# GRU and expert layer on one core: input product and b_hn written into PSUM by ScalarE and VectorE instead of being added by TensorE

## The chip, the cores and the metric

One core of a Trainium2 chip runs the whole kernel. The time is the device time of one execution in microseconds (us), median of several runs. TensorE (PE in the profile) multiplies into PSUM, VectorE (DVE), ScalarE (ACT) and GpSimd (POOL) work element by element, SyncE (SP) issues most DMAs. The engines run side by side, each through its own list of instructions in order, and wait for each other through semaphores.

## The reference

A GRU runs over x (4 sequences of 512 steps, width D = 512), its states pass through a layer of 4 experts, and x is added:

```python
def cell(h, x):
    gi = x @ W_ih + b_ih
    gh = h @ W_hh + b_hh
    i_r, i_z, i_n = jnp.split(gi, 3, axis=-1)
    h_r, h_z, h_n = jnp.split(gh, 3, axis=-1)
    r = jax.nn.sigmoid(i_r + h_r)
    z = jax.nn.sigmoid(i_z + h_z)
    n = jnp.tanh(i_n + r * h_n)
    h_new = (1.0 - z) * n + z * h
    return (h_new, h_new)
...
# each token: softmax over the 2 best of 4 experts; each expert takes its 512
# best-scored tokens: y = gelu(tok @ W1[e]) @ W2[e] * p, scattered back by addition
x = x + _L0_ffn_ref(_L0_cond_ref(cond, x, W_ih, W_hh, b_ih, b_hh), Wg, bg, W1, W2)
```

h_n holds its own bias b_hn, the last third of b_hh, which is inside the product with r.

## The kernel before

**Recurrence.** Each of the 4 sequences is cut into 16 segments of 32 steps, and all 64 segments run side by side as 64 columns (COLS). 8 steps of approach (BURN), then 32 steps, then 32 again whose states count: 72 steps, i = 0 to 71. A step needs gates = W_hh x state: 512 inputs are KD = 4 blocks k of 128 partitions, the outputs are 4 blocks j times 3 gates g (r, z, n). Block j of the gates has a PSUM bank of its own, `gate_ps[:, j, g, :]`, 192 of its 512 columns.

Numbers are split into a high and a low f16 part. In **rough** steps (i < ROUGH = 20) only high x high is multiplied: 48 products of 64 columns. In **exact** steps the list ORDER gives (HIGH, j, k), six products (high and low weights times the state's high part), and (LOW, j, k), three (high weights times its low part): 144 products in an order written by hand. TensorE's `unit` issues them, waiting for `high_ready` and `low_ready`/`last_low_ready` of block k. Its last product of block j raises `gates_mm`.

**Input product.** x W_ih is made in four chunks of 8 steps, 12 tiles of 128x512 each (m = 0 to 3 for r, 4 to 7 for z, 8 to 11 for n). The first chunk comes from f32 products before step 0. The rest is made by 432 f16 **fills** of 512 columns, spread over the steps up to 22 (`fill`, 18 a step; in rough steps 13, 2, 2 and 1 ahead of each k). ScalarE takes each tile out of PSUM (`keep_tile`). The n gates go into `gi` as f32. The r and z gates go to the ring `gi_full`, and VectorE splits them into two f16 parts, `gi_rz`, with `rz_high` (L1128) and `rz_low` (L1135).

**Adding it.** In each step TensorE's `inject` (L469, L472) opens each bank: the diagonal matrix `diag` (the scale) times gi_rz's high part of r and z (128 columns), in exact steps also times its low part, and `bhn_parts` times `bhn_unit` (64 columns) for b_hn. `inject(j)` waits for the reset of block j of the step before (`rn_done`), which is the last reader of the bank. In rough steps b_hn is added by VectorE's reset (L1248, three operands); in exact ones reset is L1245.

**The state.** ScalarE: sigmoid of r and z of block j (L779), tanh (L784), in the order sig 0, 1, 2, tanh 0, 1, sig 3, tanh 2, 3. VectorE, in an order written by hand (`exact`, `rough`): `reset` (r times h_n), `candidate_in` (L1253), `one_less_z` (L1257), `blend` (L1264, the new state's high part), in exact steps `keep_state` (L1269, the f32 state) and the low part of blocks 2 and 3 (`low_part`, L1288). GpSimd: `carry` (L952, z times old state) and the low part of blocks 0 and 1 (L960). `other_work` puts further VectorE work behind a step's list: x_low (L1146), whh_low (L1211, at the steps of WHH_AT), the splits of the input product, and the router's weights in step 10. ScalarE takes the tiles out behind its step, and in steps 29 to 40 and 45 to 48 squares a piece of W1 for its peak (L799).

**After the recurrence** come the router, a search for each expert's best tokens, and the experts; the change touches there only which PSUM banks two small results use.

Lines the prediction names besides: L434 and L424 are the first tiles' f32 products, L451 the fills, L459 the gate products, L479 the router's logits, L740 and L745 `keep_tile`, L753 `first_tile_high`, L1179 the diagonal.

Of the kernel before, what the change touches and what calls it, by code (L numbers as in the profile page):

```python
# [23 lines left out]
P = 128  # L24
# [12 lines left out]
def gru_moe(nc, x, x_t, cond_t, w_ih, w_hh, b_ih, b_hh, b_hn, wg, bg, w1, w2, hs_rows, out):  # L37
# [18 lines left out]
    with ExitStack() as ctx:  # L56
# [3 lines left out]
        def sem(name):  # L60
# [12 lines left out]
        gi_rz = big[:, :].bitcast(F16).rearrange("p (n j q) -> p n j q", n=NC_, j=KD)[:, :, :, 0:4 * GCOLS].rearrange(  # L73
            "p n j (i g c) -> p n j i g c", i=2, g=2)
# [58 lines left out]
        diag = sb("diag", [P, P], BF16)  # L133
# [38 lines left out]
        def of_first(q):  # L172
# [61 lines left out]
        lg_sum = ps[:, 4, L * 2 * E:2 * L * 2 * E].rearrange("p (l e) -> p l e", l=L)  # L234
        lg_again = ps[:, 5, 0:NT * E].rearrange("p (n e) -> p n e", n=NT)
        gate_ps = ps[:, 0:4, 0:3 * COLS].rearrange("p j (g c) -> p j g c", g=3)

        names = """small_loaded out_init consts_pool consts_dve bias_ready
             gi_mm gi_high gi_low gi_kept diag_ready sig_done gates_known gi_known x_known wih_high wih_split whh_high x_high x_split peak_ready peak_known chain whh_ready zh_done warmed high_ready state_done low_ready last_low_ready gates_mm rn_done
            candin_ready tanh_done ocand_done start_saved check_a worst_ready worst_mm flag_ready  # L240
            gru_over turned bhn_clear bhn_loaded bhn_split wg_split lg_mm lg_kept sq_done probs_in probs_stored group_made rows_copied rows_stored steps_made exp_in exp_done
# [1531 lines left out]
```

## Time and profile before

| | us |
|---|---|
| time, median of 3 runs | 836.3 (836.11 to 837.08) |
| the profiled execution | 836.27 |
| its span, first to last instruction | 834.5 |
| TensorE busy, matmuls | 803.0 (96%) |
| VectorE busy | 619.8 (74%) |
| ScalarE busy | 421.1 (50%) |
| GpSimd busy | 179.9 (22%) |
| mean granted TensorE clock | 0.987 |

The recurrence ends at about 442 us, the experts fill the rest. "Busy" of TensorE counts each matmul from its start to a modelled end, so matmuls overlap. In a timeline a row merges neighbouring instructions of a kind: start, time from the first's start to the last's end, and their number. [brackets] at the end of a row give the engine's idle time before it and who ended it.

### The profile page before, as it was taken

What the parts mean: (1) busy time and instruction counts of PE and PEld (TensorE: products, weight loads), DVE (VectorE), ACT (ScalarE), POOL (GpSimd) and SP (SyncE); (2) the same over time, 40 slices, a digit from 0 to 9 for tenths busy, and PEclk for the clock granted to TensorE, in tenths of its full rate; (3) what the DMA queues carried; (4) which work ended last, traced back from release to release, by engine and by line L of the source; (5) the groups of instructions that cost most, each with busy time, mean ns of one, the idle gap of its engine ahead of it and who ended that gap; (6) DMA issues with size and microseconds to landing.
All of it is one profiled execution on the core that took longest, in us unless ns stands there. A gap on an engine that the chain in (4) does not pass through costs nothing.

```text
span 834.5 us, 28320 instructions
## 1 busy us (share of the span) xinstructions
PE 803.0 (96%) x11781; PEld 528.0 (63%) x11782; DVE 619.8 (74%) x2113; ACT 421.1 (50%) x885; POOL 179.9 (22%) x459
## 2 busy tenths in 40 slices
PE   7999999999999999999995799999999999999996
PEld 3446556679999999999994444454445444444442
DVE  6979899878888888888888879767666676755300
ACT  0677666645566556554455448252835184417400
POOL 1002222123433334333330010121012101210011
PEclk9999999999999999999997899999999999999998
DMA  9810000000111010000001943471347224630022
GB/s 336 323 48 2 2 2 3 2 3 4 54 60 50 17 42 5 4 4 5 5 4 33 269 156 119 135 226 27 113 139 194 57 101 151 171 81 1 1 26 26
DMA packets 24286, 62.64 MB, mean 75 GB/s; under 512 B 4386, under 2 KB 4386, under 8 KB 22308
## 3 DMA queue, kind: packets, MB, share of 16 engines
q1 hardware_dynamic: 19312, 51.42, 18.1%
q0 software_dynamic: 3584, 8.42, 5.5%
q8 instruction: 87, 1.43, 0.7%
q10 hardware_dynamic: 1268, 1.08, 0.4%
q14 instruction: 35, 0.29, 0.1%
HBM read 52.50 MB, written 12.62 MB: 78 GB/s over the span
## 4 chain that ended last, share of the span: by engine, by line
PE 92%; DVE 5%; issue 1%; DMA 1%; ACT 0%; POOLq 0%; DVEq 0%
PE ps L459 29%; PE ps L666 20%; PE ps L680 20%; PE ps L451 10%; PE ps L469 3%; PE ps L434 3%; PE ps L424 2%; PE ps L600 1%; PE ps L653 1%; DVE big L1541 1%; PE ps L472 1%; DMA wa<-in_x_t 1%; DVE halves L1264 1%; DVE wa L1253 1%; PE ps L644 0%
## 5 line engine op out<-in xcount | busy, mean ns | idle before, releaser
L459 PE MATMUL ps<-halves,wa 128*128 128x64 f16 x8448 | 289.1, 193 | 1.4 <-DVE halves L1264 1.2
L459 PEld LDWEIGHTS ps<-halves,wa 128*128 128x128 f16 x8448 | 271.2, 98 | 20.2 <-DVE halves L1264 4.2
L680 PE MATMUL ps<-big 128*128 128x512 f16 x768 | 166.9, 379 | 0.0
L666 PE MATMUL ps<-hx,big 128*128 128x512 f16 x768 | 166.9, 379 | 0.0
L779 ACT ACTIVATE wa<-ps,un_gates 128x128 f32<-128x128 f32 x288 | 100.1, 365 | 111.0 <-PE ps L459 100.6
L680 PEld LDWEIGHTS ps<-big 128*128 128x128 f16 x768 | 75.1, 98 | 89.9
L666 PEld LDWEIGHTS ps<-hx,big 128*128 128x128 f16 x768 | 74.8, 98 | 90.0 <-issue 0.2
L784 ACT ACTIVATE wa<-wa,un_gates 128x64 f32<-128x64 f32 x288 | 97.4, 344 | 53.0 <-DVE wa L1253 48.9
L451 PE MATMUL ps<-hx,wb 128*128 128x512 f16 x432 | 106.9, 379 | 1.2 <-issue 1.1
L861 ACT ACTIVATE hx<-ps,un_hid_in 128x512 f32<-128x512 f32 x64 | 43.6, 682 | 109.2 <-PE ps L666 106.9
L1264 DVE SCALAR_TENSOR_TENSOR halves<-ocand,neg_scale,wa 128x64 f16<-128x64 f32 (+1 forms) x288 | 80.6, 280 | 4.4 <-issue 0.5
L1495 DVE SCALAR_TENSOR_TENSOR big<-wa,scale,big 128x2048 f16<-128x2048 f32 x28 | 65.3, 2350 | 21.1 <-ACT big L847 21.1
L1245 DVE TENSOR_TENSOR wa<-ps,wa 128x64 f32<-128x64 f32 x208 | 45.9, 221 | 43.4 <-ACT wa L779 43.4
L1253 DVE TENSOR_TENSOR wa<-wa,big 128x64 f32<-128x64 f32 x288 | 71.6, 249 | 5.1
L1629 DVE SCALAR_TENSOR_TENSOR big<-hx,hid_scale,big 128x512 f16<-128x512 f32 x64 | 47.8, 750 | 35.2 <-ACT big L864 29.0
L847 ACT ACTIVATE big<-wa,scale 128x2048 f16<-128x2048 f32 x28 | 54.8, 1988 | 34.1 <-DVEq L1483 34.1
L1441 DVE TENSOR_REDUCE chunk_peak<-wa 128x1 f32<-128x2048 f32 x28 | 62.3, 2279 | 4.5 <-DMA wa<-in_w 4.5
L469 PE MATMUL ps<-big,diag 128*128 128x128 f16 x496 | 63.5, 219 | 0.8 <-DVE wa L1245 0.4
L1257 DVE SCALAR_TENSOR_TENSOR ocand<-wa 128x64 f32<-128x64 f32 x288 | 63.5, 220 | 0.0
L451 PEld LDWEIGHTS ps<-hx,wb 128*128 128x128 f16 x432 | 37.9, 98 | 35.8 <-issue 1.9
L1018 POOL DMA_INDIRECT out<-hx,idx_out x16 | 29.0, 1815 | 136.1 <-DVE hx L1635 136.1
L952 POOL TENSOR_TENSOR wa<-wa,hx 128x64 f32<-128x64 f32 x128 | 40.9, 320 | 79.9 <-ACT wa L779 75.2
(221 smaller groups left out, 791.4 us busy)
## 6 DMA issues: line engine op xcount, KB each, us to landing
wa<-in_w SPq DMA_DIRECT2D x28, 1024.0 KB, 5.2
hs_rows<-big SPq DMA_DIRECT2D x8, 512.0 KB, 6.3
big<-in_w_hh SPq DMA_DIRECT2D x4, 768.0 KB, 19.6
wb<-in_w SPq DMA_DIRECT2D x12, 256.0 KB, 2.6
big<-in_w_ih SPq DMA_DIRECT2D x2, 1024.0 KB, 12.5
hx<-in_x_t SPq DMA_DIRECT2D x2, 1024.0 KB, 16.5
big<-in_w_ih ACTq DMA_DIRECT2D x2, 512.0 KB, 6.6
wa<-in_x_t SPq DMA_DIRECT2D x2, 512.0 KB, 6.2
```

The source lines that it names most:

```text
L451: mm = pe.matmul(ps[:, gi_bank(tile), :], wih_parts[:, w, k, m * P:(m + 1) * P], x_parts[:, q, t, k, :], start=(left == 0), stop=(left == ...
L459: mm = pe.matmul(gate_ps[:, j, g, :], whh_parts[:, k, w, (4 * g + j) * P:(4 * g + j + 1) * P], halves[:, src, k, h, :], start=False, stop= ...
L469: pe.matmul(gate_ps[:, j, 0:2, :], diag[:, :], gi_rz[:, c, j, part, :, cols], start=(part == HIGH), stop=False, skip_group_check=True)
L666: mm = pe.matmul(ps[:, m % 2, :], w1p[:, w, k, m * P:(m + 1) * P], tokT[:, t, k, :], start=(k == 0 and n == 0), stop=(k == KD - 1 and n == 2))
L680: mm = pe.matmul(ps[:, 2 + g % 2, :], hid[:, h, k, g * P:(g + 1) * P], w2p[:, w, k, :], start=(k == 0 and n == 0), stop=(k == KH - 1 and n ...
L779: act.activation(rz[:, j, :, :], gate_ps[:, j, 0:2, :], ACT.Sigmoid, scale=un_gates[:, 0:1]).then_inc(S["sig_done"], 1)
L784: act.activation(cand[:, j, :], cand_in[:, j, :], ACT.Tanh, scale=un_gates[:, 0:1]).then_inc(S["tanh_done"], 1)
L1253: dve.tensor_tensor(cand_in[:, j, :], rn[:, j, :], gi_n(j), ALU.add).then_inc(S["candin_ready"], 1)
L1257: dve.scalar_tensor_tensor(ocand[:, j, :], rz[:, j, 1, :], -1.0, cand[:, j, :], ALU.add, ALU.mult).then_inc(S["ocand_done"], 1)
L1264: dve.scalar_tensor_tensor(high_of(j), old(ocand_, j), neg_scale[:, 0:1], old(zh_, j), ALU.mult, ALU.add).then_inc(S["high_ready"], 1)
L1441: dve.tensor_reduce(chunk_peak[:, c:c + 1], stage[:, c * CHUNK:(c + 1) * CHUNK], AX.X, ALU.max, apply_absolute_value=True).then_inc(S["chu ...
L1495: dve.scalar_tensor_tensor(w_parts[which][:, LOW, cols], stage[:, cols], scale[:, which:which + 1], w_parts[which][:, HIGH, cols], ALU.mul ...
```

## The change

TensorE no longer opens the banks. The r and z input product stays f32 in `gi_rz`, written by `keep_tile` directly, two gates of a step side by side, so `gi_full`'s ring, `rz_high` and `rz_low` go, and with them `inject`, `diag` and the split of b_hn. What `inject` added is now written into the gate banks before the products, which accumulate onto it: a **seed**, two instructions, `gi_rz` times the column `seed_s` (128 columns of a block) and b_hn (64 columns).

Steps 0 to 23: VectorE writes the seeds of step i + 1 block by block at the end of its list of step i (`seed_next`, eight instructions), ahead of `other_work` in the rough steps. TensorE does all 18 fills of a rough step first, then the products block by block, j outside and k inside, each block behind `seeded_early`.

Steps 24 to 71: ScalarE writes them. Blocks 0 to 2 have two sets of banks (0 to 2 and 5 to 7) used in turn, and after its last tanh of step i ScalarE seeds blocks 0 to 2 of step i + 2 (`seed_most`, 384 and 192 elements) and block 3 of step i + 1 (`seed_last`, 128 and 64). In step 23 it seeds all that steps 24 and 25 need. The squares come behind the seeds.

```diff
-        gate_ps = ps[:, 0:4, 0:3 * COLS].rearrange("p j (g c) -> p j g c", g=3)
+        GATES = 3 * COLS
+        gate_banks = (ps[:, 0:KD - 1, 0:GATES], ps[:, 5:5 + KD - 1, 0:GATES])
+        last_gates = ps[:, KD - 1, 0:GATES]
...
-        INJECT = 2
-        ORDER = ((INJECT, 0, 0), (INJECT, 1, 0), (HIGH, 1, 0), (INJECT, 2, 0), (HIGH, 0, 0), (HIGH, 2, 0),
-                 (INJECT, 3, 0), (HIGH, 0, 1), (HIGH, 1, 1), (LOW, 1, 0), (HIGH, 2, 1), (LOW, 2, 0),
...
+        ORDER = ((HIGH, 1, 0), (HIGH, 0, 0), (HIGH, 2, 0), (HIGH, 0, 1), (HIGH, 1, 1), (LOW, 1, 0),
...
-        FILLS = (13, 2, 2, 1)
-        FILL_STEP = sum(FILLS)
+        FILL_STEP = 18
...
             def gates_rough(src, i):
-                n = filled(i)
-                for k in range(KD):
-                    fill(n + sum(FILLS[:k]), n + sum(FILLS[:k + 1]))
-                    if k == 0 and i % STEPS_C == 0:
-                        pe.wait_ge(S["gi_high"], 8 * (i // STEPS_C) + 8)
-                    pe.wait_ge(S["high_ready"], made(i) + k + 1)
-                    for j in range(KD):
-                        if k == 0:
-                            inject(j, *place(i), (HIGH,), KD * i)
-                        unit(HIGH, j, k, src, (HIGH,), k == KD - 1)
+
+                fill(filled(i), filled(i + 1))
+                for j in range(KD):
+                    pe.wait_ge(S["seeded_early"], 2 * (KD * i + j + 1))
+                    for k in range(KD):
+                        pe.wait_ge(S["high_ready"], made(i) + k + 1)
+                        unit(0, HIGH, j, k, src, (HIGH,), k == KD - 1)
...
+                    if j not in begun:
+                        begun.add(j)
+                        if early:
+                            pe.wait_ge(S["seeded_early"], 2 * (2 * half_steps + j + 1))
+                        elif j == KD - 1:
+                            pe.wait_ge(S["last_seeded"], half_steps + (2 - 2 * FILLED))
+                        elif j == ORDER[0][1]:
+                            pe.wait_ge(S["seeded"], half_steps + (2 - 2 * FILLED))
...
+            def seed_most(bank, rows_of, before):
+
+                act.wait_ge(S["rn_done"], before)
+                act.activation(gate_banks[bank][:, :, 0:2 * COLS], rows_of(slice(0, KD - 1)), ACT.Copy,
+                               scale=seed_s[:, 0:1]).then_inc(S["seeded"], 1)
+                act.activation(gate_banks[bank][:, :, 2 * COLS:GATES],
+                               bhn_s[:, 0:KD - 1].unsqueeze(2).to_broadcast([P, KD - 1, COLS]), ACT.Copy
+                               ).then_inc(S["seeded"], 1)
...
+            def seed_ahead(i):
+
+                if i + 2 < FIRST + L:
+                    seed_most(bank_of(i + 2), rows_at(i + 2), KD * (i + 2))
+                if i + 1 < FIRST + L:
+                    seed_last(rows_at(i + 1), KD * (i + 2))
...
             for i in range(FIRST + L):
-                step(KD * i)
+                step(KD * i, bank_of(i))
+                if i >= FILLED:
+                    seed_ahead(i)
...
+                if i + 1 == FILLED:
+                    act.wait_ge(S["gi_kept"], 12 * NC_)
+                    act.wait_ge(S["seeds_known"], 1)
+                    seed_most(bank_of(FILLED), rows_at(FILLED), KD * FILLED)
+                    seed_ahead(i)
...
+            def seed(i, j):
+
+                c = (i // STEPS_C + CHUNK_ORDER[0]) % NC_
+                dve.tensor_scalar(gates_of(0, j)[:, 0:2 * COLS], gi_rz[:, c, j, i % STEPS_C, :], seed_s[:, 0:1], None,
+                                  ALU.mult).then_inc(S["seeded_early"], 1)
+                dve.tensor_copy(gates_of(0, j)[:, 2 * COLS:GATES], bhn_s[:, j:j + 1].to_broadcast([P, COLS])
+                                ).then_inc(S["seeded_early"], 1)
...
-                         (low_part, 3))
+                         (low_part, 3), *((seed_next, j) for j in range(KD)))
...
-                         (one_less_z, 2), (blend, 2), (one_less_z, 3), (blend, 3), (other_work, 0))
-                for f, n in ahead:
-                    f(n)
+                         (one_less_z, 2), (blend, 2), (one_less_z, 3), (blend, 3),
+                         *((seed_next, j) for j in range(KD)), (other_work, 0))
```

## Rows read from the trace of the kernel before

**Rows 1.** The page, the chain that ended last: share of the span by engine.

```profile
PE 92%; DVE 5%; issue 1%; DMA 1%; ACT 0%; POOLq 0%; DVEq 0%
```

**Rows 2.** Busy us of each engine by stretch, granted TensorE clock, DMA.

```profile
60.00:170.00 110.00, 109.56 (x1374) 66.45 (x1371) 98.95 (x386) 72.05 (x195) 24.15 (x81) 1.00 0.01 2
170.00:202.00 32.00, 31.01 (x782) 26.36 (x780) 23.58 (x109) 14.92 (x41) 8.95 (x26) 1.00 0.02 4
202.00:260.00 58.00, 57.85 (x1814) 56.11 (x1811) 48.86 (x260) 34.48 (x108) 23.09 (x72) 1.00 0.16 50
```

**Rows 3.** Timeline of TensorE, rough steps: start us, us, engine, line, tiles, count.

```profile
61.25 2.97 PE L451 MATMUL ps<-hx,wb 128*128 128x512 f16 x13
...
66.76 2.97 PE L451 MATMUL ps<-hx,wb 128*128 128x512 f16 x13
```

**Rows 4.** Timeline of TensorE, exact steps 20 and 24.

```profile
172.03 3.84 PE L459 MATMUL ps<-halves,wa 128*128 128x64 f16 x126
...
203.00 0.28 PE L469 MATMUL ps<-big,diag 128*128 128x128 f16 x2
...
203.46 0.35 PE L459 MATMUL ps<-halves,wa 128*128 128x64 f16 x6
...
204.28 3.88 PE L459 MATMUL ps<-halves,wa 128*128 128x64 f16 x126
```

**Rows 5.** Timeline of VectorE, a rough step whose list starts late.

```profile
72.69 0.28 DVE L1248 SCALAR_TENSOR_TENSOR wa<-ps,bhn_s,wa 128x64 f32<-128x64 f32 x1
...
76.18 0.42 DVE L1128 CAST big<-gi_full 128x512 f16<-128x512 f32 x1
76.63 0.69 DVE L1135 TENSOR_TENSOR big<-gi_full,big 128x512 f16<-128x512 f32 x1
```

**Rows 6.** Timeline of VectorE, exact steps 24 and 25.

```profile
203.84 0.29 DVE L1264 SCALAR_TENSOR_TENSOR halves<-ocand,neg_scale,wa 128x64 f16<-128x64 f32 x1
...
206.76 0.22 DVE L1245 TENSOR_TENSOR wa<-ps,wa 128x64 f32<-128x64 f32 x1 [0.76 <-ACT wa L779]
...
210.59 0.41 DVE L1288 TENSOR_TENSOR halves<-carried,halves 128x64 f16<-128x64 f32 x2
211.75 0.23 DVE L1245 TENSOR_TENSOR wa<-ps,wa 128x64 f32<-128x64 f32 x1 [0.76 <-ACT wa L779]
```

**Rows 7.** Timeline of ScalarE, an exact step with a square.

```profile
229.36 0.35 ACT L784 ACTIVATE wa<-wa,un_gates 128x64 f32<-128x64 f32 x1 [0.60 <-DVE wa L1253]
229.62 0.61 ACT L799 ACTIVATE wa<-wb 128x512 f32<-128x512 f32 x1
230.14 0.19 ACT L799 ACTIVATION_READ_ACCUMULATOR wa<-wb 128x1 f32 x1
231.32 1.16 ACT L779 ACTIVATE wa<-ps,un_gates 128x128 f32<-128x128 f32 x3 [0.99 <-PE ps L459]
```

**Rows 8.** The page, costliest groups: busy us, mean ns, idle before.

```profile
L847 ACT ACTIVATE big<-wa,scale 128x2048 f16<-128x2048 f32 x28 | 54.8, 1988 | 34.1 <-DVEq L1483 34.1
```

**Rows 9.** Timeline of TensorE, where the fills begin.

```profile
50.57 8.15 PE L451 MATMUL ps<-hx,wb 128*128 128x512 f16 x37 [1.14 <-issue]
```

**Rows 10.** VectorE's groups by line and shape, rough steps: busy us, mean ns.

```profile
L1248 DVE SCALAR_TENSOR_TENSOR wa<-ps,bhn_s,wa 128x64 f32<-128x64 f32 x76 | 21.1, 278 | 6.6 <-ACT wa L779 6.5
...
L1211 DVE SCALAR_TENSOR_TENSOR wa<-big,scale,wa 128x512 f16<-128x512 f32 x12 | 9.0, 750 | 0.0
```

**Rows 11.** Timeline of VectorE, the diagonal before step 0.

```profile
50.38 0.29 DVE L1179 TENSOR_SCALAR diag<-ident,un_gi 128x128 bf16<-128x128 f32 x1
```

**Rows 12.** Timeline of TensorE, first products of steps 20 and 23.

```profile
167.05 4.06 PE L451 MATMUL ps<-hx,wb 128*128 128x512 f16 x18
...
191.71 0.28 PE L469 MATMUL ps<-big,diag 128*128 128x128 f16 x2
```

**Rows 13.** Timeline of TensorE, behind the router's search.

```profile
474.07 2.53 PE L644 MATMUL ps<-tok_group,gi_full 128*128 128x4 f16 x16 [2.50 <-DVE gi_full L1599]
```

**Rows 14.** TensorE's busy us and granted clock behind that.

```profile
475.00:480.00 5.00, 5.00 (x19) 0.50 0.94 333
```

More of the change, by code:

```diff
@@ L463, in unit @@
                     mm.then_inc(S["gates_mm"], 1)
-            def inject(j, c, cols, parts, steps):
-                pe.wait_ge(S["rn_done"], steps + j + 1)
-                for part in parts:
-                    pe.matmul(gate_ps[:, j, 0:2, :], diag[:, :], gi_rz[:, c, j, part, :, cols],
-                              start=(part == HIGH), stop=False, skip_group_check=True)
-                if LOW in parts:
-                    pe.matmul(gate_ps[:, j, 2, :], bhn_parts[:, j * P:(j + 1) * P], bhn_unit[:, :], start=False,
-                              stop=False, skip_group_check=True)
             def logits(i):
@@ L542, in _, with run @@
             logits(FIRST + L).then_inc(S["lg_mm"], 1)
-            def run(base, low_base, steps):
+            def run(base, low_base, half_steps):
                 for c in range(NC_):
@@ L806, in _, with run @@
                     x_high(i // STEPS_C + 1, i % STEPS_C)
-            def run(steps, n):
-                with act.Fori(0, n // 2) as i:
-                    for u in range(2):
-                        step(steps + 8 * i + 4 * u)
+                if i + 1 == FILLED:
[3 more added lines that the diff above has]
+                    seed_ahead(i)
+            def run(steps):
+                for c in range(NC_):
+                    with act.Fori(0, STEPS_C // 2) as i:
+                        for u in range(2):
+                            base = steps + KD * STEPS_C * c + 8 * i + 4 * u
+                            rows_of = lambda j: gi_rz[:, c, j, bass.ds(2 * i + u, 1), :].rearrange(
+                                "p j o q -> p (j o) q" if isinstance(j, slice) else "p o q -> p (o q)")
+                            seed_most(1 - u, rows_of, base + KD)
+                            seed_last(rows_of, base + KD)
+                            step(base, 1 - u)
             def exponents(count):
@@ L1206, in whh_low @@
+            for j in range(KD):
+                seed(0, j)
             def whh_low(n):
@@ L1228, in w1_peak, with step @@
                 dve.tensor_reduce(peak[:, W1:W1 + 1], sq[:, :], AX.X, ALU.max).then_inc(S["w_peak"], 1)
-            def step(gi_n, after, src, base, low, moved=False, ahead=(), between=(), bias_added=True):
+            def step(gi_n, after, src, base, low, bank, moved=False, between=(), following=None):
                 dst = 1 - src
@@ L1337, in _ @@
                     after = lambda j, i=i: hs[:, j, i - FIRST + 1, :]
-                ahead, between = [], []
-                if i < FILLED:
-                    for t in range(split_by(i - 1), split_by(i)):
-                        if TILES[t][1] < 8:
-                            (ahead if s == STEPS_C - 1 else between).append((rz_high, t))
-                            (ahead if i == FILLED - 1 else between).append((rz_low, t))
+                between = []
                 if 1 <= s <= KD and q < 2:
@@ L1351, in _ @@
                     between.append((w1_peak, 0))
-                step(lambda j, c=c, cols=cols: gi[:, c, j, 2, cols], after, i % 2, KD * i, i >= ROUGH - 1, moved, ahead, between,
-                     i >= ROUGH)
+                step(lambda j, c=c, cols=cols: gi[:, c, j, 2, cols], after, i % 2, KD * i, i >= ROUGH - 1, bank_of(i), moved,
+                     between, i + 1 if i + 1 < FILLED else None)
             def run(steps):
```

174 lines of the change are left out of this document (62 added, 112 removed).

## The prediction

> **Names.** Step i is step i of the recurrence, i = 0 to 71; steps 0 to 19 are rough, 20 to 71 exact. E(i) is the start of the last gate product of step i on TensorE. A "slot" is the time from one instruction's start to the next one's on the same engine when nothing is waited for.
>
> **What bounds the kernel now.** I read the chain that ended last first, then the busy shares by stretch, then the timelines of TensorE, VectorE and ScalarE over single steps. The chain is 92% TensorE [rows 1], which invites the sum "every product removed is time gained". The stretches [rows 2] say the same: TensorE is busy for 109.6 of 110 us in the rough steps and for 57.9 of 58 in exact ones. The busy figure of a matmul is a pipelined 0.19 us while products start 0.03 us apart, so it hides gaps of 0.1 us. One has to look inside a step.
>
> Rough step [rows 3]: 13 fills in 2.97 us, the last of them 0.38, are 0.216 us each from start to start. 126 products of 64 columns in 3.84 us [rows 4], the last 0.19, are 0.0292 each. The period is 66.76 - 61.25 = 5.51 us. 18 fills are 3.89, 48 products 1.40, so the four input products take the rest, 0.22. There is no gap: TensorE bounds these steps. VectorE is close behind. Its 16 instructions for the state run from 72.69 to 76.18 when it starts late, 3.49 us, then come rz_high and rz_low, 0.42 and 0.69 busy [rows 5], and a piece of other splitting.
>
> Exact step [rows 4]: here a gap shows. Step 20's last 126 products, for which VectorE is nowhere late, take 3.84 us. Step 24's and all later ones take 3.88. So 0.04 us is waited for in every steady step, in the middle of the products, and 0.2 us more between the input products and the first unit (203.00 plus two groups at 0.14, then 203.46). What TensorE waits for in the middle is the low half of the state's last quarter. VectorE starts a step's list with reset 0 at 206.76 and issues the last pair of low parts at 210.59 for 0.41 us [rows 6]; in between it is never idle. The circle is: VectorE's list, 4.24 us to the end of low part 3 at 211.00; then 0.75, of which 0.03 until TensorE starts the unit (LOW, 0, 3), 0.06 until that completes gate 0, and the rest for sigmoid 0 and its two hand-overs; then reset 0 again at 211.75. 4.99 us, the step. VectorE's list therefore sets the exact steps together with TensorE, and the input products lie in TensorE's wait for the state.
>
> **The change, part by part.**
>
> *Exact steps 25 to 71 (47).* 12 products go (8 of 128 columns, 4 of 64). A group of three starts 0.14 behind the one before (two of 128 columns at twice 0.0292, one of 64), the four are 0.56 us. Without them TensorE waits for high part 0 just the same, then for high part 1 (blend 1, 203.84 to 204.13 [rows 6], used from 204.28 now [rows 4]), then for low parts 2 and 3. The unit (LOW, 0, 3) begins when low part 3 is there, at the same place of the circle. All 0.56 us turns into waits: **0**. If the low parts were not what is waited for, high part 1 would still hold the step to 0.12 below the present one, 4.88.
>
> *ScalarE's seeds.* Each of these steps gets four ACTIVATEs of 384, 192, 128 and 64 elements. A tanh of 64 elements with its scale from memory is 0.35 us and the next instruction starts after 0.26; a square of 512 with an immediate scale is 0.61 [rows 7]. 2048 elements with a scale from memory are 1.988 [rows 8], so an element is (1.988 - 0.35) / 1984 = 0.00083 us, and the fixed part is 0.29 with the scale from memory and 0.19 without. The four are 0.61, 0.35, 0.40 and 0.24; with 0.09 of overlap each, slots of 0.52, 0.26, 0.31 and 0.15: 1.24 us. Writing PSUM from ScalarE is in no row; I bound the four by 1.05 (0.05 cheaper each) and 1.6 (0.09 dearer each). From the last tanh to the next sigmoid 0 there are 231.32 - 229.36 = 1.96 us. From tanh 3 a plain step needs 0.26 + 1.24 = 1.50 and keeps 0.46. In 16 steps (29 to 40, 45 to 48) a square with its accumulator read lies there too, 0.52 + 0.19 = 0.71 [rows 7]: 2.21 us, 0.25 too many. Sigmoid 0 is on the circle without slack, so each costs 0.25: **+4.0** (bounds +1.0 and +9.8). Queued behind the square are the three sigmoids, and VectorE's whole list waits for them.
>
> The rows hold no ACTIVATE into PSUM. The Trainium skill ("ScalarE: Activation LUTs", "Step-by-step: what each stage is for") says an ACTIVATE into PSUM is faster than one into SBUF. No row of before shows it; by it the term would lie at the lower bound, +1.0.
>
> *The start.* rz_low 0 to 3 leave VectorE's list and three rz_high leave ScalarE's; TensorE's idle of 1.14 us before the fills [rows 9] was for the last x_low, which now ends some 1.8 us earlier, so the fills begin at 49.43. 42 of them and 48 products put E(0) at 49.43 + 9.07 + 1.40 = 59.9, against 61.25 [rows 3].
>
> *Rough steps.* TensorE alone would need 3.89 + 1.40 = 5.29. VectorE gives up rz_high and rz_low but takes eight seeds, behind the blends and ahead of its other work. Its state list gets shorter since reset becomes a two-operand instruction, 0.22 [rows 6] for 0.278 [rows 10]; with the hand-overs 3.49 becomes 3.30. A seed of 128 elements is a multiply by a column into PSUM. The nearest rows are the diagonal, 128 elements in 0.29 [rows 11], and three-operand instructions: 0.278 for 64 elements, 0.750 for 512 [rows 10], so 0.00105 us an element and 0.345 for 128. Slots are 0.08 under the busy time: 0.21 or 0.27. The copy of 64 has a slot of 0.14 (0.22 busy, as a reset). A pair is 0.35 to 0.41, and 0.49 if writing PSUM costs the overlap of the first. I take 0.41, the element rate that most rows have; four pairs are 1.63 (bounds 1.3 and 2.0). Other work, whh_low or x_low at 0.75 busy [rows 10], is a slot of about 0.70 in 18 steps, double in step 1, and 1.54 more in step 10: 15.5 in all. So VectorE needs 3.30 + 1.63 + 0.70 = 5.63 in a usual step, more than TensorE's 5.29 and more than 5.51. It becomes the bound, and its other work now stands between the seeds and the next reset.
>
> The row of the diagonal alone would allow two elements a cycle. The Trainium skill ("VectorE: DVE Perf Modes", "Why PSUM operands drop a tier") says that an fp32 instruction with a PSUM operand runs at one. By the row four pairs are 1.40, by the page 1.63.
>
> Sum: the gates of a rough step are now completed one after the other over the last 1.05 us before E, so VectorE's list of 3.30 begins some 0.3 us before E(0) and, with waits for the later gates, ends near 3.1 behind it, at 63.0. Eighteen more steps at 3.30 + 1.63 are 88.7, their other work 14.7, the shifted step 7 0.4: 166.8. Seeds (1.63), hand-over (0.08) and the last unit's 12 products (0.35) put E(19) 2.06 later, 168.9. The fills of step 20 follow it; before they began at 167.05 [rows 12]. **+1.9**, start included (bounds -6.5, TensorE-bound, and +9).
>
> *Steps 20 to 24.* The exact list on VectorE is free again at 210.59 + 0.33 [rows 6], 2.95 us behind E(25) = 203.00 + 4.99 - 0.03, and the seeds of the next step come only behind it. TensorE's first units need pairs 1 and 0, 0.82 more and 0.05 for the hand-over: 3.80 behind E. 18 fills (3.89) cover that, 12 fills (2.59) before step 22 don't, and nothing covers it before step 23. A step's 144 products are 4.2. Step 20: its list starts 0.29 behind E(19), so 0.29 + 4.16 + 0.87 + 4.25 = 9.6. Step 21: 3.89 + 4.2 = 8.1. Step 22: 3.80 + 4.25 = 8.05. The three are 25.75 against 191.71 - 167.05 = 24.7 [rows 12]. Step 23: 8.05. Step 24 is seeded by ScalarE, behind tanh 3 of step 23 (its slot ends 1.7 behind E), two slots and the hand-over: its products start 2.6 behind E and it takes 6.8. The two are 14.85 against 203.00 - 191.71 = 11.3, in which the splits rz_high and rz_low made TensorE wait. Together **+4.6** (bounds +3.5 and +6).
>
> *The clock.* TensorE stands idle for about 3.7 us before step 23. In this trace an idle of 2.50 us [rows 13] was followed by a granted clock of 0.50, the 1.2 GHz level, for over 4 us of work [rows 14]. Half of 4.2 us is **+2.1** (bounds 0 and +5, were it to happen before step 24 too).
>
> The router and the experts are unchanged. Total: 1.9 + 4.6 + 2.1 + 4.0 = +12.6. The profiled execution took 836.27 us (span 834.5 and 1.8 around it), the median of the three runs is 836.3, so one baseline serves: **848.9 us**.
>
> **Rivals.**
>
> *A. TensorE does bound the exact steps.* Then 47 x 0.56 = 26 us go, less what ScalarE allows: at 4.45 a step the room of 1.96 is 1.41 and its 1.50 sets 4.53, so 22 us: 827. For it: the chain [rows 1]. Against: the 0.04 us wait in each steady step [rows 4]. It decides from 12.6 / 47 = 0.27 us a step. Chance 0.08.
>
> *B. The seeds on VectorE are cheap.* At 1.3 us for four pairs VectorE needs 5.3 and TensorE bounds the rough steps: E(19) = 59.9 + 19 x 5.29 = 160.4, 8.5 us below my sum, and the total is 840, 838 with the clock kept up, 835 with ScalarE at its lower bound as well. Chance 0.12.
>
> *C. Seeds are dear on both engines.* 2.0 us on VectorE adds 7.4, 1.5 on ScalarE adds 4.2: 860. Chance 0.12.
>
> *D. Only the high parts hold the exact steps*, at 4.88: 47 x 0.12 = 5.6 less, 843. Chance 0.06.
>
> *E. The clock falls in the exact steps.* TensorE would idle 0.7 us of 5. At the lower level 144 products take 8.4 and a step over 8.4, +3.4 us in each of 47: 1009. Against it: the stretch from 170 to 202 us, in which TensorE idles for 0.99 us, has a clock of 1.00 [rows 2]. The Trainium skill ("TensorE: Matmul & The Clock Gate", "HAM oscillation — how this bites in real kernels") describes a clock that falls again and again where bursts of matmuls are parted by waits; the trace so far sides against it for waits this short. Chance 0.02.
>
> **How the numbers follow.** The forecast has 0.60, by itself 841 to 857. Below 837 lie A and a part of B (0.11), above 860 E and half of C (0.08): range 837 to 860. 0.2% (1.7 us) is about what a measurement can tell. Faster by more: A and 0.02 of B, 0.10. Within: 0.05 from B's lower end. Slower: 0.85.
>
> **What would show it.** Exact plain steps still 5.0 us apart with TensorE waiting at two or three places; square steps 0.2 to 0.3 longer; rough steps near 5.6 with VectorE never idle; a hole of some 3.7 us before step 23 and 2.6 before step 24; a clock of 0.50 behind the hole. Wrong if exact steps fall clearly under 5.0, or rough steps come every 5.3 us.

## The result and the profile after

The changed kernel took 843.48 us (842.39 to 845.57), the kernel before beside it 836.48: a ratio of 1.0086 (95% interval 1.0063 to 1.0109). It is slower by 7.0 us; the forecast was 12.6 slower. The profiled execution took 842.39 us with a span of 840.6, 6.1 more than the profiled one of before. Its parts, read at the same places of both traces:

| | forecast | measured |
|---|---|---|
| start and rough steps, to the fills of step 20 | +1.9 | +0.1 |
| steps 20 to 24, clock left out | +4.6 | +4.4 |
| low clock in step 23 | +2.1 | +1.55 |
| exact steps 25 to 71, products and squares | +4.0 | -0.4 |
| router and experts | 0 | +0.5 |

The page's chain that ended last, which had 92% on TensorE [rows 1] (the exact steps take 4.99 us in both kernels, so these shares alone say little of what bounds them):

```profile
PE 61%; DVE 28%; ACT 6%; issue 3%; DMA 1%; POOLq 0%; DVEq 0%
```

TensorE's timeline, steps 20 to 24 (start, us, engine, line, tiles, count, idle before it and who ended it); the last row is step 26:

```profile
167.17 4.06 PE L446 MATMUL ps<-hx,wb 128*128 128x512 f16 x18
172.18 4.36 PE L454 MATMUL ps<-halves,wa 128*128 128x64 f16 x144 [0.96 <-DVE ps L1177]
...
188.40 4.36 PE L454 MATMUL ps<-halves,wa 128*128 128x64 f16 x144 [1.16 <-DVE ps L1177]
196.51 5.91 PE L454 MATMUL ps<-halves,wa 128*128 128x64 f16 x144 [3.74 <-DVE ps L1177]
204.86 4.36 PE L454 MATMUL ps<-halves,wa 128*128 128x64 f16 x144 [2.45 <-DVE halves L1246]
...
214.50 4.69 PE L454 MATMUL ps<-halves,wa 128*128 128x64 f16 x144 [0.29 <-DVE halves L1246]
```

The fills of step 20 begin at 167.17 where they began at 167.05 [rows 12]. Then four waits stand there, of 0.96, 1.16, 3.74 and 2.45 us; the first three end with a seed of VectorE (L1177 is its copy of b_hn into PSUM). Beside the fourth the profile names a blend of step 23, which ends at 204.71; but step 24's first products need the first block only, whose blend was done at 202.64, and ScalarE's seed for blocks 0 to 2, the row below, ends at 204.72. So ScalarE's seed ends that wait, as forecast; e1's trace names it. Step 23's 144 products take 5.91 us and not 4.36. The steady step's take 4.69: 0.33 us of waiting inside, and 0.29 before it. The next row of that kind is 4.99 us on (219.49), as before.

```profile
204.41 0.31 ACT L747 ACTIVATE ps<-bhn_s 128x192 f32<-128x192 f32 x1
```

TensorE's granted clock there (stretch, length, busy us and counts by engine, clock, DMA):

```profile
196.50:199.00 2.50, 2.49 (x60) 2.50 (x61) 0.62 (x4) 0.00 (x0) 0.00 (x0) 0.66 0.02 7
199.00:202.00 3.00, 3.00 (x81) 3.00 (x79) 0.97 (x5) 1.32 (x5) 0.80 (x3) 0.72 0.00 0
...
209.00:440.00 231.00, 217.49 (x6752) 205.04 (x6748) 191.32 (x1017) 181.28 (x586) 90.12 (x276) 1.00 0.08 23
```

Behind the wait of 3.74 us a part of the work runs at the lower level, 1.2 GHz. Behind the wait of 2.45 it doesn't, and the exact steps keep 1.00 although TensorE waits 0.6 us in each.

VectorE's timeline, a rough step:

```profile
76.32 0.22 DVE L1222 TENSOR_TENSOR wa<-ps,wa 128x64 f32<-128x64 f32 x1
...
79.70 0.35 DVE L1175 TENSOR_SCALAR ps<-big,seed_s 128x128 f32<-128x128 f32 x1
79.96 0.22 DVE L1177 COPY ps<-bhn_s 128x64 f32<-128x64 f32 x1
80.08 0.34 DVE L1175 TENSOR_SCALAR ps<-big,seed_s 128x128 f32<-128x128 f32 x1
...
81.22 0.74 DVE L1139 SCALAR_TENSOR_TENSOR hx<-hx,scale 128x512 f16<-128x512 f32 x1
81.88 0.22 DVE L1222 TENSOR_TENSOR wa<-ps,wa 128x64 f32<-128x64 f32 x1
```

The list for the state is 3.38 us (3.30 foreseen), the four pairs 81.22 - 79.70 = 1.52 (1.63 foreseen; a pair has slots of 0.26 and 0.12), other work 0.66 (0.70): 5.56, with no gap on VectorE longer than 0.11 us.

ScalarE's timeline, the first exact step with a square, which answers to [rows 7]:

```profile
235.49 0.35 ACT L779 ACTIVATE wa<-wa,un_gates 128x64 f32<-128x64 f32 x1 [0.60 <-DVE wa L1235]
235.74 0.57 ACT L745 ACTIVATE ps<-big,seed_s 128x384 f32<-128x384 f32 x1
236.25 0.31 ACT L747 ACTIVATE ps<-bhn_s 128x192 f32<-128x192 f32 x1
236.50 0.35 ACT L754 ACTIVATE ps<-big,seed_s 128x128 f32<-128x128 f32 x1
236.79 0.20 ACT L756 ACTIVATE ps<-bhn_s 128x64 f32<-128x64 f32 x1
236.94 0.61 ACT L796 ACTIVATE wa<-wb 128x512 f32<-128x512 f32 x1
237.46 0.19 ACT L796 ACTIVATION_READ_ACCUMULATOR wa<-wb 128x1 f32 x1
237.55 1.05 ACT L774 ACTIVATE wa<-ps,un_gates 128x128 f32<-128x128 f32 x3
...
240.48 0.35 ACT L779 ACTIVATE wa<-wa,un_gates 128x64 f32<-128x64 f32 x1 [0.60 <-DVE wa L1235]
```

From tanh 3 to sigmoid 0 it is 2.06 us where a plain step has 1.96: sigmoid 0 comes 0.10 late. Yet tanh 3 to tanh 3 is 240.48 - 235.49 = 4.99.

VectorE's timeline, reset 0 and the first one_less_z of the plain step ahead of it and of this one:

```profile
232.85 0.22 DVE L1222 TENSOR_TENSOR wa<-ps,wa 128x64 f32<-128x64 f32 x1 [0.76 <-ACT wa L774]
...
233.87 0.23 DVE L1239 SCALAR_TENSOR_TENSOR ocand<-wa 128x64 f32<-128x64 f32 x1
...
237.93 0.22 DVE L1222 TENSOR_TENSOR wa<-ps,wa 128x64 f32<-128x64 f32 x1 [0.84 <-ACT wa L774]
...
238.86 0.23 DVE L1239 SCALAR_TENSOR_TENSOR ocand<-wa 128x64 f32<-128x64 f32 x1
```

Reset 0 is 5.08 behind the one before, but one_less_z 0 is 4.99 behind its own: the five instructions between them take 0.93 us instead of 1.02, because small waits among them close up.

### The profile page after: what moved, and what is told of

The parts are those of the page before. It is cut to its first block, busy times and chain, and to the rows that moved or that the text cites. A ratio compares the mean times of both kernels' runs of the same rounds, so it can differ in the third digit from the quotient of the medians.

```text
span 840.6 us, 27308 instructions
## 1 busy us (share of the span) xinstructions
PE 788.2 (94%) x11077; PEld 501.6 (60%) x11078; DVE 617.1 (73%) x2237; ACT 476.7 (57%) x1072; POOL 190.5 (23%) x459
## 4 chain that ended last, share of the span: by engine, by line
PE 61%; DVE 28%; ACT 6%; issue 3%; DMA 1%; POOLq 0%; DVEq 0%
PE ps L643 20%; PE ps L657 20%; PE ps L454 12%; DVE wa L1235 6%; DVE halves L1246 5%; DVE wa L1222 4%; PE ps L429 3%; DVE ocand L1239 3%; DVE ps L1175 3%; ACT wa L774 2%; PE ps L419 2%; PE ps L446 2%; ACT wa L796 1%; DVE ps L1177 1%; DVE wa L1189 1%
## 5 line engine op out<-in xcount | busy, mean ns | idle before, releaser
L454 PE MATMUL ps<-halves,wa 128*128 128x64 f16 x8448 | 275.8, 194 | 24.6 <-DVE halves L1246 15.0
L454 PEld LDWEIGHTS ps<-halves,wa 128*128 128x128 f16 x8448 | 259.8, 98 | 47.7 <-DVE halves L1246 20.3
L774 ACT ACTIVATE wa<-ps,un_gates 128x128 f32<-128x128 f32 x288 | 103.8, 365 | 56.3 <-PE ps L454 47.3
L1222 DVE TENSOR_TENSOR wa<-ps,wa 128x64 f32<-128x64 f32 x288 | 63.0, 219 | 57.1 <-ACT wa L774 57.1
L446 PE MATMUL ps<-hx,wb 128*128 128x512 f16 x432 | 97.0, 379 | 0.1
L446 PEld LDWEIGHTS ps<-hx,wb 128*128 128x128 f16 x432 | 40.7, 98 | 46.4 <-issue 0.6
L960 POOL TENSOR_TENSOR wa<-wa,halves 128x64 f32<-128x64 f32 x80 | 34.9, 455 | 84.5 <-ACT wa L774 84.4
```

The lines of the kernel that those rows point to most:

```text
L446: mm = pe.matmul(ps[:, gi_bank(tile), :], wih_parts[:, w, k, m * P:(m + 1) * P], x_parts[:, q, t, k, :], start=(left == 0), stop=(left == ...
L454: mm = pe.matmul(gates_of(bank, j)[:, g * COLS:(g + 1) * COLS], whh_parts[:, k, w, (4 * g + j) * P:(4 * g + j + 1) * P], halves[:, src, k, ...
L774: act.activation(rz[:, j, :, :], gates_of(bank, j)[:, 0:2 * COLS].rearrange("p (g c) -> p g c", g=2), ACT.Sigmoid, scale=un_gates[:, 0:1]) ...
L960: pool.tensor_tensor(zh[:, j, :], rz[:, j, 1, :], before(j), ALU.mult).then_inc(S["zh_done"], 1)
L1222: dve.tensor_tensor(rn[:, j, :], gates_of(bank, j)[:, 2 * COLS:GATES], rz[:, j, 0, :], ALU.mult).then_inc(S["rn_done"], 1)
```

## The experiments

The theory after the result: (1) in the exact steps VectorE's list to the end of low part 3 sets the period; (2) in the rough steps it is VectorE's whole list with the seeds; (3) steps 20 to 24 pay for seeds that stand behind everything else, and once more by the clock. Rivals: TensorE still bounds the exact steps and another thing took the 26 us back; ScalarE does; the clock is an affair of the whole stretch. A difference in us below is between medians; "changed" stands for 843.5.

**e1, the holes filled.** Dummy products of 512 columns ahead of steps 22, 23 and 24:

```
+ KEPT_WARM = {22: 5, 23: 16, 24: 10}
+ if i in KEPT_WARM:
+     pe.wait_ge(S["gi_kept"], 45)
+     for _ in range(KEPT_WARM[i]):
+         pe.matmul(ps[:, 4, :]..., onesb, onesb..., start=True, stop=True)
```

> The changed kernel, with products nobody reads (512 columns, another bank) in TensorE's waits: 5 ahead of step 22, 16 ahead of step 23, 10 ahead of step 24. Clock theory: the granted clock stays at 1.00 over steps 22 to 24, step 23's 144 products take 4.36 us instead of 5.91, the holes keep their length, and the time falls by 1.5 us to some 841. The changed kernel's spread from run to run (842.4 to 845.6) should shrink too, if it is the clock's. Rival, that the long step 23 has another cause (its waits for high and low parts): it stays at 5.9 and the time at 843.

841.57 us, ratio 1.0057 (1.0040 to 1.0074). TensorE's timeline, steps 23 and 24:

```profile
192.82 3.62 PE L515 MATMUL ps<-onesb 128*128 128x512 bf16 x16
196.73 4.36 PE L455 MATMUL ps<-halves,wa 128*128 128x64 f16 x144 [0.29 <-DVE ps L1183]
...
203.55 4.36 PE L455 MATMUL ps<-halves,wa 128*128 128x64 f16 x144 [0.30 <-ACT ps L753]
```

The products of step 23 begin where they did (196.73 for 196.51), so the hole is not TensorE's doing, and take 4.36 for 5.91. What the idle time had cost was the clock: 1.55 us, 1.9 by the medians. The four times of e1 lie within 0.7 us, those of the changed kernel within 3.2; that fits a loss by the clock that differs from one execution to the next (e8 has a trace with a larger one).

**e2 and e3, low part 2 by GpSimd**, in the changed kernel and in the one before. VectorE's list loses one of two low parts, the circle of theory (1):

```
- LOW_BY = "PPDD"
+ LOW_BY = "PPPD"
-  (one_less_z, 3), (keep_state, 2), (blend, 3), (keep_state, 3), (low_part, 2),
+  (one_less_z, 3), (keep_state, 2), (blend, 3), (keep_state, 3),
```

> The changed kernel, with the low part of block 2 made by GpSimd instead of VectorE in all exact steps. Theory (VectorE's list up to low part 3 sets the exact steps, TensorE has 0.5 us of waits in each): low part 3 comes 0.13 earlier, the next limit is high part 1, so steps of 4.88 instead of 4.99 and 47 x 0.11 = 5 us less: 838. Rival 1, TensorE bounds the exact steps: no change, 843. Rival 2, GpSimd's extra work slows VectorE's own instructions on the way they share: 843 to 848.

> The kernel before, with the same move of low part 2 to GpSimd. Theory: TensorE waits there in the middle of a step for 0.04 us only, so at most 47 x 0.04 = 1.9 us can come off: 834.5 to 836. If it gained as much as the changed kernel does by the same move (5 us), TensorE's input products would be free in both, and what the change saves on TensorE would be worth nothing even with a shorter VectorE list.

Both slower: 847.16 (ratio 1.0131, 1.0114 to 1.0148) and 841.28 (1.0057, 1.0040 to 1.0073), 3.7 us over the changed kernel and 4.4 over the one before. VectorE's timeline of e2:

```profile
350.98 0.23 DVE L1222 TENSOR_TENSOR wa<-ps,wa 128x64 f32<-128x64 f32 x1 [0.76 <-ACT wa L774]
...
354.03 0.35 DVE L1239 SCALAR_TENSOR_TENSOR ocand<-wa 128x64 f32<-128x64 f32 x1
...
354.70 0.27 DVE L1251 SCALAR_TENSOR_TENSOR hx<-ocand,neg_scale,wa 128x64 f32<-128x64 f32 x1
355.07 0.23 DVE L1270 TENSOR_TENSOR halves<-hx,halves 128x64 f16<-128x64 f32 x1
356.05 0.22 DVE L1222 TENSOR_TENSOR wa<-ps,wa 128x64 f32<-128x64 f32 x1 [0.76 <-ACT wa L774]
```

Two costs stand against the gain. Low part 3 waits for keep_state 3 to finish (355.07, 0.10 after its end), which low part 2 had covered. And one_less_z 3 takes 0.35 us where it takes 0.21, beside GpSimd's extra work. The list was meant to get shorter and got longer: from reset 0 to the end of low part 3 it is 355.30 - 350.98 = 4.32 us, where the changed kernel has 4.23 (e8 shows its rows), and the period is 5.07 for 4.99. The period follows that end, as theory (1) says, but the move did not test its gain. That both kernels react alike, one with the input products and one without, speaks for one bound in both.

**e4 and e10, more work on ScalarE.** One or two further copies, into a spare SBUF tile, ahead of the seeds (e4: 192 and 64 elements, slots 0.25 and 0.15; e10: the one of 64):

```
  def seed_ahead(i):
+     act.wait_ge(S["spared"], spares[0])
+     act.activation(spare[:, 0:KD - 1, :], bhn_s..., ACT.Copy).then_inc(S["spared"], 1)   # e4 alone
+     act.activation(spare[:, KD - 1, :], bhn_s..., ACT.Copy).then_inc(S["spared"], 1)
```

> The changed kernel, with two more ScalarE copies of b_hn (192 and 64 elements, into SBUF) ahead of the seeds in steps 23 to 71, 0.41 us of ScalarE a step. Theory (from tanh 3 to sigmoid 0 there are 1.96 us and 0.10 of slack behind them; tanh, seeds and square take 0.26 + 1.20 + 0.61 = 2.06): plain steps 0.26 + 1.20 + 0.41 = 1.87, no change, 4.99; the 16 square steps 2.47, 5.40 each, so 6.6 us more in all: 850. Without any slack, as the prediction had it, square steps would take 5.50. Rival, that ScalarE is not near the limit even with squares: no change.

> The changed kernel with one more copy of 64 elements (0.24 us, a slot of 0.15) on ScalarE ahead of the seeds. With two copies (0.40) the 16 steps that have a square took 5.54 us, the others 4.99; without any all take 4.99 and the first square step 5.08. Theory (in square steps ScalarE's own loop, from tanh 3 over seeds and square to sigmoid 0 and back to tanh 3, is as long as VectorE's, so every added nanosecond shows): 5.54 - 0.25 = 5.29 in square steps, 16 x 0.30 = 4.8 us, 848.3. Rival (there is about 0.1 us of slack left that the square didn't use, and the two copies also changed the order of arrivals): 5.04 to 5.14, 844.5 to 846. Rival (no slack at all but no jump either, the loop is 4.99 + 0.15): 5.14, 845.9.

e4 took 852.3 us (ratio 1.0184, 1.0165 to 1.0202), e10 847.36 (1.0140, 1.0121 to 1.0160). ScalarE's timeline of e10, a square step:

```profile
240.63 0.35 ACT L786 ACTIVATE wa<-wa,un_gates 128x64 f32<-128x64 f32 x1 [0.80 <-DVE wa L1242]
...
245.93 0.35 ACT L786 ACTIVATE wa<-wa,un_gates 128x64 f32<-128x64 f32 x1 [0.80 <-DVE wa L1242]
```

Plain steps stay at 4.99 in both: there ScalarE has room for 0.40 us. Square steps become 5.54 and 5.28 to 5.30: 16 x 0.55 = 8.8 and 16 x 0.30 = 4.8, the medians say 8.8 and 3.9. (One of the 16 takes 5.65 in the changed kernel, 5.90 in e4 and still 5.65 in e10, so the steps themselves give 8.5 and 4.5.) The step follows the dose one to one (0.25 for 0.25), but the line through both points meets 5.14 at no dose, where 4.99 is measured. So the square steps stand at an edge: up to the seeds and the square as they are nothing shows, and 0.15 us more costs 0.30. The extra 0.15 goes with an order of arrivals (candidate_in 1 takes 0.37 us for 0.22 and tanh 1 waits 0.19 for it, in both). The traces show GpSimd beside it: its third multiply begins 0.02 to 0.04 us ahead of candidate_in 1 in e10 and e4 (some 238.56 for 238.59 in e10), in the changed kernel 0.09 behind it (238.67 for 238.58), and 0.37 - 0.22 is the 0.15. It fits what GpSimd did to one_less_z 3 in e2, but it was not tried.

**e5, ScalarE seeds steps 20 to 23**, behind tanh 3 of the step before; VectorE keeps steps 0 to 19:

```
- between, i + 1 if i + 1 < FILLED else None)
+ between, i + 1 if i + 1 < ROUGH else None)
+ if ROUGH <= i + 1 < FILLED:
+     seed_early(i + 1)
```

> The changed kernel, but the banks of steps 20 to 23 are written by ScalarE (four copies, 1.20 us, behind tanh 3 of the step before) and VectorE writes those of steps 0 to 19 only. Theory (the holes before steps 22 and 23 are VectorE's list plus two seed pairs, and the low clock in step 23 follows from the hole of 3.74 us): the first two copies end 0.25 + 0.50 + 0.25 us behind the start of tanh 3, so the hole before step 23 becomes about 2.45 us as it is before step 24, step 23's products take 4.36 us and not 5.91, and step 20's and 22's fill waits go: 5.0 to 5.6 us less than the changed kernel, about 837. Rival (the low clock comes from the light load of the whole stretch and not from the long hole): step 23 stays at 5.9 us, about 839. Rival (the place of the seeds doesn't matter since the products of these steps wait for the state): no change, 842.4.

839.29 us, ratio 1.0030 (1.0018 to 1.0042), 4.2 less than changed. TensorE's timeline, steps 22 to 24:

```profile
183.42 2.75 PE L446 MATMUL ps<-hx,wb 128*128 128x512 f16 x12
186.04 4.36 PE L454 MATMUL ps<-halves,wa 128*128 128x64 f16 x144
192.85 5.91 PE L454 MATMUL ps<-halves,wa 128*128 128x64 f16 x144 [2.45 <-ACT ps L768]
201.21 5.73 PE L454 MATMUL ps<-halves,wa 128*128 128x64 f16 x144 [2.45 <-DVE halves L1265]
```

The waits before steps 20 and 22 are gone and the one before 23 is 2.45, as the theory said. But both steps behind a wait of 2.45 us now run partly at the low clock, which my expectation excluded. Step 23 does so behind a single wait: TensorE's timeline marks none from 167.24 to 190.40, and the granted clock was 1.00 up to 194 us and 0.50 behind that. In the changed kernel the same wait before step 24, behind a step that had itself run partly at the low level, left the clock alone. So the length of the wait does not decide, and no run here shows what does. The first rival of the expectation met both of its numbers, 5.9 us and 839. Its reason, the light load of the whole stretch in place of one long hole, stays open: e1 and e9 fill the holes and with them the stretch, so they show that TensorE's idle time there costs the clock, and not which part of it.

The two slow steps cost 1.55 + 1.37 = 2.9 us in this execution, where the changed kernel lost 1.55, so by the traces the new place of the seeds is worth some 1.4 us more than the 4.2. The profiled execution is one of the slower ones of e5, 1.3 us above its median.

**e6, VectorE's seeds merged**: four instructions where there were eight (384 and 192 elements, then 128 and 64).

```
+ dve.tensor_scalar(gate_banks[0][:, :, 0:2 * COLS], gi_rz[:, c, 0:KD - 1, i % STEPS_C, :], seed_s[:, 0:1], None, ALU.mult)
+ dve.tensor_copy(gate_banks[0][:, :, 2 * COLS:GATES], bhn_s[:, 0:KD - 1]...)
  (and the same two for last_gates)
```

> The changed kernel, but VectorE writes the banks of steps 0 to 23 with four instructions (three units' 384 and 192 elements, then the last unit's 128 and 64) where it had eight. From the slots of 0.255 for 128 and 0.13 for 64 elements and 0.00105 us an element for a multiply by a column, the four are about 1.17 us and the eight 1.53. Theory (from the fifth rough step on VectorE's list of 3.38 + 1.53 + other work sets the period of 5.56 us): it needs 5.2 now, TensorE's fills and products set 5.29, and 14 steps give back 0.27 each and the hole of step 10 a part: 4 to 5 us less than the changed kernel, about 838.5. Rival (the period is set by TensorE and the hand-over at the step's start, since the first gate's bank now comes later than before): 842.4 or up to 2 more.

839.26 us, ratio 1.0032 (1.0019 to 1.0045), 4.2 less. VectorE's timeline:

```profile
79.96 0.61 DVE L1176 TENSOR_SCALAR ps<-big,seed_s 128x384 f32<-128x384 f32 x1
80.48 0.35 DVE L1178 COPY ps<-bhn_s 128x192 f32<-128x192 f32 x1
80.75 0.34 DVE L1182 TENSOR_SCALAR ps<-big,seed_s 128x128 f32<-128x128 f32 x1
81.00 0.22 DVE L1184 COPY ps<-bhn_s 128x64 f32<-128x64 f32 x1
81.12 0.74 DVE L1139 SCALAR_TENSOR_TENSOR hx<-hx,scale 128x512 f16<-128x512 f32 x1
```

The seeds take 81.12 - 79.96 = 1.16 us for 1.52, and the rough step falls to TensorE's 5.29. Step 20's fills begin at 162.93 instead of 167.17. Theory (2) holds: in the rough steps VectorE was the bound. On TensorE the products of two steps start 86.27 - 80.98 = 5.29 us apart.

**e7, the products put back.** Twelve idle products per step of about the removed sizes, at their old places in TensorE's list:

```
+ for n, (h, j, k) in enumerate(ORDER):
+     if not early:
+         for _ in range((2, 1, 0, 1)[n] if n < 4 else 0):
+             for cols in (127, 127, COLS):
+                 pe.matmul(ps[:, 4, 384:384 + cols], onesb[:, :], onesb[:, 0:cols], start=True, stop=True)
```

> The changed kernel, with products of the removed ones' number and about their size put back in steps 24 to 71, at their old places in TensorE's list (two groups of three ahead of the first unit, one behind the first unit, one behind the third; 127, 127 and 64 columns; they read a constant and write to columns that nothing uses). 12 of them were 0.56 us a step in the kernel before. Theory (the removed products lay in TensorE's waits for the high and low parts, VectorE's list sets the step): the step stays 4.99, in all 842.4 and at most 1 us more. Rival A of the forecast (TensorE bounds the step): up to 0.56 us in each of 48 steps, 869. Half-way rival (a part of the 0.56 us, the group ahead of the second high part, no longer fits since the seeds changed the arrival of the gates): 0.1 to 0.2 a step, 847 to 852.

843.39 us, ratio 1.0081 (1.0068 to 1.0095), 0.1 beside the changed kernel's 843.48. TensorE's timeline:

```profile
301.66 3.88 PE L454 MATMUL ps<-halves,wa 128*128 128x64 f16 x126
...
306.65 3.88 PE L454 MATMUL ps<-halves,wa 128*128 128x64 f16 x126
```

The pattern of [rows 4] is back, 3.88 us for 126 products included, and the step is still 4.99 (306.65 - 301.66). 576 products cost nothing. Rival A is out: TensorE does not bound these steps, however full its list looks.

**e8, one more copy on VectorE**, of 64 elements, between keep_state 3 and low part 2 of steps 24 to 71:

```
+ def spare_copy(_):
+     dve.wait_ge(S["spared"], base // KD - FILLED)
+     dve.tensor_copy(spare[:, :], bhn_s[:, 0:1].to_broadcast([P, COLS])).then_inc(S["spared"], 1)
- (blend, 3), (keep_state, 3), (low_part, 2),
+ (blend, 3), (keep_state, 3), (spare_copy, 0), (low_part, 2),
```

> The changed kernel with one more copy of 64 elements into a spare tile on VectorE, between keep_state 3 and low_part 2 of steps 24 to 71 (a slot of 0.13 us). Theory (the circle of the exact step is VectorE's list to the end of low part 3, then the unit that uses it, sigmoid 0 and reset 0): 0.13 us a step in 47 steps, 6 us more than the changed kernel, 848.5 and a period of 5.12. Rival D of the forecast (the high parts hold the step, at 4.88, and the low parts come 0.1 us early): at most 0.02 to 0.03 a step, 843.5. Rival (tanh 0 behind sigmoid 2 on ScalarE closes the circle): no change, 842.4.

845.25 us, ratio 1.0110 (1.0092 to 1.0128), 1.8 over changed: neither of my numbers. VectorE's timeline of the changed kernel, then that of e8:

```profile
212.81 0.23 DVE L1222 TENSOR_TENSOR wa<-ps,wa 128x64 f32<-128x64 f32 x1 [0.76 <-ACT wa L774]
...
216.63 0.41 DVE L1270 TENSOR_TENSOR halves<-carried,halves 128x64 f16<-128x64 f32 x2
217.80 0.22 DVE L1222 TENSOR_TENSOR wa<-ps,wa 128x64 f32<-128x64 f32 x1 [0.76 <-ACT wa L774]
```

```profile
218.23 0.18 DVE L1272 COPY spare<-bhn_s 128x64 f32<-128x64 f32 x1
218.34 0.35 DVE L1277 TENSOR_TENSOR halves<-carried,halves 128x64 f16<-128x64 f32 x2
219.44 0.23 DVE L1223 TENSOR_TENSOR wa<-ps,wa 128x64 f32<-128x64 f32 x1 [0.76 <-ACT wa L775]
```

The copy has a slot of 0.11 us, but the pair of low parts behind it shrinks from 0.41 to 0.35: low part 3 had been waiting for keep_state 3, and the copy fills that wait. The pair ends 0.04 to 0.05 later in the step and the period is 5.03, 0.04 more; 47 x 0.04 = 1.9, the 1.8 of the medians. The profiled execution took 847.01, 1.8 above the median: there step 23's products, behind a wait of 3.75 us (3.74 in the changed kernel), took 6.62 us and not 5.91. The period follows the end of low part 3, as theory (1) says, and from there to the next reset 0 it is 0.76 (217.80 - 217.04) and 0.75 us (219.44 - 218.69). I had priced the copy, not what it does to that end.

**e9, the three together**: e5, e6 and ten idle products ahead of steps 23 and 24.

> The changed kernel with three edits together: ScalarE writes the banks of steps 20 to 23 (alone 4.2 us less than the changed kernel), VectorE's seeds of steps 0 to 19 are four instructions in place of eight (alone 4.2 us less), and 10 idle products of 512 columns stand ahead of steps 23 and 24. With the seeds moved alone both holes of 2.45 us were there and steps 23 and 24 took 5.91 and 5.73 us. Theory (the three costs are separate, and the clock falls for the idle of the two holes together): steps 23 and 24 take 4.36 us, 2.9 us less, and the sum is 843.5 - 4.2 - 4.2 - 2.9 = 832.2, faster than the kernel before (836.9) by 0.5%. Rival (the gains overlap, as the rough steps end earlier but the state of step 20 then waits for something else): 835 to 837. Rival (the clock falls elsewhere instead): 834.5 to 835.5.

832.67 us (831.86 to 833.29), ratio 0.9952 (0.9938 to 0.9965): faster than the kernel before by 4.2 us and than the changed one by 10.8. TensorE's timeline, steps 23 and 24:

```profile
187.16 4.36 PE L455 MATMUL ps<-halves,wa 128*128 128x64 f16 x144 [0.30 <-DVE halves L1278]
191.36 2.32 PE L515 MATMUL ps<-onesb 128*128 128x512 bf16 x10
193.97 4.36 PE L455 MATMUL ps<-halves,wa 128*128 128x64 f16 x144 [0.29 <-DVE halves L1278]
```

Steps 23 and 24 take 4.36 again, and the sum of the single gains, 832.2, was met within 0.5. So the loss of the change lay in the rough steps' list and in steps 20 to 24, and the time can be had back in both; e9's two holes are still there, filled with products that nobody reads.

## Why the prediction was right, and where its sizes were off

**Exact steps, the products: right.** Their removal was put at 0, and e7 shows it from the other side. (The unit of [rows 4] at 203.46, called step 24's there, is step 25's; no term changes by it.) The measured time lies on rival D's 843, by chance: D wants exact steps of 4.88, and they take 4.99. Low part 3 is on the circle: e8 moved the period by just what it moved its end, and from there to reset 0 it is 0.75 to 0.76 us in both kernels. Only the last piece was drawn too simply, as the squares showed.

**The squares: the step that failed, +4.0 for 0.** It is most of the error: without this term the forecast is 844.9. Two things were wrong in "0.52 + 0.19" and "sigmoid 0 is on the circle without slack". The accumulator read is 0.19 busy but its slot is 0.09 (237.46 to 237.55): I had taken the busy time for the slot, which I had not done with any other instruction. That leaves 0.10 to 0.15. And sigmoid 0 has that much room: reset 0 came 0.09 late and one_less_z 0 on time. One_less_z 0 waits for tanh 0, which stands behind sigmoid 2 on ScalarE, and tanh 0 was on time too (238.50, 0.95 behind sigmoid 0 where a plain step has 1.05). Sigmoid 2 waits for gate 2, complete 27 products after gate 0, so the circle closes through gate 2 and tanh 0, and reset 0 lies 0.09 us beside it. The lateness did not add up: the first square step is 5.08 from reset 0 to reset 0, the next ones 4.99. That the wait for gate 2 is the closing one is read from these rows; no run took it away. e4 and e10 show that the fear was sound by itself, a further 0.15 us costs 0.30 in each.

**ScalarE's seeds: 1.20 for 1.24.** The Trainium skill ("ScalarE: Activation LUTs", "Step-by-step: what each stage is for") calls an ACTIVATE into PSUM the faster one. The runs agree, by 0.04 us: a copy of 192 elements is 0.31 into PSUM and 0.35 into SBUF (e4).

**Start and rough steps: mechanism right, +1.9 for +0.1.** E(0) was 59.42 (59.9 foreseen). The first two periods were still TensorE's, 5.28 and 5.29, the third 6.16, and the usual one after that was 5.56 for 5.63. The seeds were 1.52 for 1.63, priced by a three-operand row. The rate of one element a cycle for fp32 with PSUM, which the Trainium skill gives ("VectorE: DVE Perf Modes", "Why PSUM operands drop a tier"), fits the slope: (0.61 - 0.345) / 256 = 0.00104 us an element, the rate that I took from [rows 10]. The fixed part was smaller. Rival B (TensorE bounds the rough steps) needed 1.25 us for the four pairs; e6 made it come true with 1.16.

**Steps 20 to 24: right, +4.4 for +4.6**, with holes of 3.74 (3.7) and 2.45 (2.6).

**The clock: right place, 1.55 for 2.1.** Only part of step 23 ran at the lower level; half of the whole step had been charged. e1 shows the cause, idle time ahead of it. That the long hole is what did it, as the forecast had it, is not shown: e5 has the same 5.91 us behind 2.45. The Trainium skill ("TensorE: Matmul & The Clock Gate", "HAM oscillation — how this bites in real kernels") warns of a clock that falls between bursts. Here it fell in step 23, in e5 in step 24 too, and nowhere in the 47 steps of the changed kernel with 0.6 us of waits.

**The sum.** The total was 6.5 us too high in the profiled executions: 4.4 of it the squares and a little of the exact steps, 1.8 the rough steps, 0.5 the clock, 0.2 steps 20 to 24, less 0.5 in the router and the experts. That last one was put at nothing. In the low-clock stretch behind the router's search, 16 products of 512 columns take 6.24 us where the kernel before takes 5.90; why is not known. The -0.4 of the exact steps is no more than that part varies by: from step 25's first product to step 71's there are 230.64 us in the changed kernel and 231.25 in e9, whose list there is the same.

## What to carry to other kernels

Products that lie in a wait are worth nothing to take away, and the work that replaces them must then be free too: it was in the exact steps, where ScalarE had room, and was not in the rough steps, where VectorE was close behind TensorE and became the bound, or where the seeds stood last in its list. Price the end of the instruction that others wait for, not the slot of the one added: the same copy may fill a dependency wait. A hole on TensorE may cost twice, its length and the clock behind it, and a few idle products are a cheap test of the second.

## What the runs showed of the hardware

- The clock fell behind a wait of 3.74 us (changed), behind a single one of 2.45 us and behind another of 2.45 us one step later (e5), but not behind one of 2.45 us that came after the slow step 23 (changed). Behind a wait of 3.74 to 3.77 us the low clock cost 1.55 us in most traces and 2.26 in e8's. With the waits filled it stayed at 1.00 (e1, e9).
- ScalarE's accumulator read is 0.19 us busy, but the next instruction starts 0.09 behind it.
- A dependent instruction on VectorE started 0.10 us after the end of the one it needed (e2, 354.97 to 355.07), even on the same engine.
- VectorE's instruction of 0.21 us on SBUF took 0.35 while GpSimd had one more low part to work on (e2); between 210 and 440 us the mean of that line went from 218 to 251 ns.
